# Expert loop of a mixture-of-experts kernel: up projection computed transposed, weights stationary and rows moving, without transposes of the activation

## What is computed

```python
flat = hidden_states.reshape(B * S, H)             # 1536 tokens, H = 192
probs = softmax(flat @ router_w.T)                 # E = 8 experts
topk_probs, topk_idx = top_k(probs, 2)
h = einsum('th,eih->tei', flat, w1)                # up:   192 -> 512
h = silu(h)
outs = einsum('tei,ehi->teh', h, w2)               # down: 512 -> 192
combined = (outs at topk_idx * balanced).sum(axis=1)
```

## Time and profile before

| | us |
|---|---|
| median of 3 runs | 404.68 (402.76 to 408.04) |
| span of the profiled execution | 391.4 |
| first gather of the expert loop | 271.49 |
| first up projection | 276.82 |
| start of the first scatter | 286.54 |
| start of the last scatter | 373.51 |

### The profile page before, as it was taken

How to read it: one execution, slowest core, us unless ns; L and a number is a source line. 1 busy time by engine, 2 the same in 40 slices (tenths; PEclk the granted TensorE clock), 3 DMA queues, 4 the chain that set the end, 5 groups by cost and what they waited for, 6 DMA issues and landing times.

```text
span 391.4 us, 7182 instructions
## 1 busy us (share of the span) xinstructions
PE 254.3 (65%) x2269; PEld 182.2 (47%) x2270; DVE 261.5 (67%) x763; ACT 184.2 (47%) x396; POOL 128.6 (33%) x133
## 2 busy tenths in 40 slices
PE   5986658776443334546656579512899999999800
PEld 3444434444343333435555457501376667667600
DVE  2115568997388898899949976597355555655566
ACT  1131325898798587657526321400255456445401
POOL 3000232554025423303300000012667876866321
PEclk9998556999555565555555555555699999999975
DMA  6000032000004512220100000000211211110046
GB/s 182 6 0 0 1 124 93 3 0 2 2 2 107 121 68 83 80 82 2 32 1 3 7 23 3 30 30 10 62 51 51 69 45 57 53 43 27 26 146 216
DMA packets 12973, 18.98 MB, mean 48 GB/s; under 512 B 3259, under 2 KB 10850, under 8 KB 12434
## 3 DMA queue, kind: packets, MB, share of 16 engines
q1 hardware_dynamic: 9922, 13.90, 11.8%
q0 software_dynamic: 3024, 4.73, 4.1%
HBM read 14.68 MB, written 5.41 MB: 51 GB/s over the span
## 4 chain that ended last, share of the span: by engine, by line
PE 43%; DVE 39%; issue 7%; ACT 6%; DMA 3%; SPq 1%; POOL 0%; DVEq 0%; POOLq 0%; ACTq 0%
DVE at_half L1434 6%; DVE atm L1397 5%; PE bank L891 4%; PE bank L880 3%; PE bank L904 2%; PE bank L906 2%; PE bank L905 2%; PE bank L741 2%; PE bank L876 2%; PE bank L578 2%; PE bank L879 2%; PE bank L878 2%; PE bank L877 2%; DVE v L1320 2%; PE bank L546 2%
## 5 line engine op out<-in xcount | busy, mean ns | idle before, releaser
L480 POOL TENSOR_TENSOR wx<-early,wx 128x1536 f16<-128x1536 f32 (+2 forms) x8 | 28.7, 3584 | 62.6 <-ACT wx L1075 62.6
L1116 ACT ACTIVATE qk<-bank 128x512 f32<-128x512 f32 x31 | 18.5, 597 | 65.1 <-PE bank L880 65.1
L487 POOL DMA_INDIRECT qk<-x_rows,tok_row x32 | 38.6, 1206 | 24.1 <-DVE tok_row L1550 12.8
L741 PE MATMUL bank<-vg,at_half 128*128 128x17 f16 x432 | 13.5, 176 | 40.8 <-DVE at_half L1434 40.8
L492 POOL DMA_INDIRECT y_rows<-qk,dst_row x31 | 31.4, 1013 | 21.7 <-DVE qk L1589 14.9
L1583 DVE COPY qk<-bank 128x512 f16<-128x512 f16 x31 | 13.2, 425 | 33.2 <-PE bank L891 33.2
L741 PEld LDWEIGHTS bank<-vg,at_half 128*128 128x128 f16 x432 | 12.5, 104 | 42.4 <-DVE at_half L1434 27.7
L904 PE MATMUL bank<-wx,qk 128*128 x124 | 30.5, 246 | 0.7 <-DVE qk L1583 0.5
L906 PE MATMUL bank<-wx,qk 128*128 x124 | 30.5, 246 | 0.0
L905 PE MATMUL bank<-wx,qk 128*128 x124 | 30.5, 246 | 0.0
L1056 ACT ACTIVATE at_half<-atm 128x384 f16<-128x384 f32 x48 | 22.5, 518 | 12.9 <-DVE atm L1397 12.9
(11 more groups left out here) (297 smaller groups left out, 737.0 us busy)
## 6 DMA issues: line engine op xcount, KB each, us to landing
early<-in_w SPq DMA_DIRECT2D x4, 768.0 KB, 4.2
early<-in_w1a SPq DMA_DIRECT2D x2, 1024.0 KB, 6.0
early<-in_w1b SPq DMA_DIRECT2D x4, 512.0 KB, 6.3
x_rows<-xr SPq DMA_DIRECT2D x12, 96.0 KB, 1.7
v<-y_rows SPq DMA_DIRECT2D x4, 288.0 KB, 5.0
qk<-y_rows SPq DMA_DIRECT2D x4, 288.0 KB, 5.3
out<-h SPq DMA_DIRECT2D x4, 288.0 KB, 2.9
at_half<-in_wq SPq DMA_DIRECT2D x1, 704.0 KB
```

Source lines behind the costliest of these rows:

```text
L480: pool.tensor_tensor(low, w, high, ALU.subtract).then_inc(s_w_low, 1)
L487: pool.indirect_dma_start(xg[:, i % 4, :], None, x2_dram, bass.IndirectOffsetOnAxis(ap=tok_row[:, i:i + 1], axis=0), bounds_check=NTOK - 1 ...
L741: mm = pe.matmul(bank[6][:, hh * VE:(hh + 1) * VE], at_half[:, a_, i, g, :], vg[:, t * H + hh, v, :], start=(c == 0 and hh == 0 and a_ == ...
```

## The change

`up` is computed transposed. For each of the four blocks of 128 hidden units, the block of weights is stationary and the 128 rows of the slot move: 20 matmuls of 128 columns in place of 5 of 512. The result has hidden units in the partitions and rows in the columns, which is the layout that `down` needs as its stationary operand. So `act_t`, `high_t` and `low_t` go, with `actT`, three semaphores, and PSUM banks 6 and 7 of this stage. `down` takes its operands from `acth` and `actl`. As these buffers are now read by `down`, the second silu and the subtraction of slot i wait for down(i - 2) (`s_down_mm`), and `down` waits for the subtraction. The low half of w1b is computed for 128 partitions, and the last product of `up` uses all 128 (which adds low x low for the last 64 inputs).

```diff
-        parts = {"w1a": (FI, P, W1H, W1L), "w1b": (FI, D - P, W1BH, W1BL), "w2": (MC * D, P, W2H, W2L)}
+        parts = {"w1a": (FI, P, W1H, W1L), "w1b": (FI, P, W1BH, W1BL), "w2": (MC * D, P, W2H, W2L)}
...
                 k %= 2
-                o_ = bank[2 + k][:, :]
-                pe.matmul(o_, xe[:, k, 0:P], w[:, W1H:W1H + FI], start=True, stop=False)
-                pe.matmul(o_, xe[:, k, P:2 * P], w[:, W1H:W1H + FI], start=False, stop=False)
-                pe.matmul(o_, xe[:, k, 0:P], w[:, W1L:W1L + FI], start=False, stop=False)
-                pe.matmul(o_, xe[:, k, 2 * P:3 * P], w[:, W1BH:W1BH + FI], start=False, stop=False)
-                pe.matmul(o_, xe[0:D - P, k, 2 * P:3 * P], w[0:D - P, W1BL:W1BL + FI], start=False, stop=True).then_inc(s_up_mm, 1)
-
-            def act_t(i, k, first=False):
+                for m in range(MC):
+                    o_ = bank[2 + k][:, m * P:(m + 1) * P]
+                    c = m * P
+                    pe.matmul(o_, w[:, W1H + c:W1H + c + P], xe[:, k, 0:P], start=True, stop=False)
+                    pe.matmul(o_, w[:, W1H + c:W1H + c + P], xe[:, k, P:2 * P], start=False, stop=False)
+                    pe.matmul(o_, w[:, W1L + c:W1L + c + P], xe[:, k, 0:P], start=False, stop=False)
+                    pe.matmul(o_, w[:, W1BH + c:W1BH + c + P], xe[:, k, 2 * P:3 * P], start=False, stop=False)
+                    mm = pe.matmul(o_, w[:, W1BL + c:W1BL + c + P], xe[:, k, 2 * P:3 * P], start=False, stop=True)
+                mm.then_inc(s_up_mm, 1)
+
+            def down(i, k, w, first=False):
                 pe.wait_ge(s_low_ready, i + 1)
-                if not first:
-                    pe.wait_ge(s_actT_high, i)
-                    pe.wait_ge(s_actT_low, i)
-                k %= 2
-                for v, half in enumerate((acth, actl)):
-                    ps = bank[6 + v][:, 0:FI // 2].bitcast(F16)
-                    for m in range(MC):
-                        mm = pe.transpose(ps[:, m * P:(m + 1) * P], half[:, k, m * P:(m + 1) * P], ident16[:])
-                mm.then_inc(s_actT_mm, 1)
...
-                    pe.matmul(o_, actT[:, k, 0, c], w[:, W2H + d:W2H + d + D], start=(m == 0), stop=False)
-                    pe.matmul(o_, actT[:, k, 1, c], w[:, W2H + d:W2H + d + D], start=False, stop=False)
-                    mm = pe.matmul(o_, actT[:, k, 0, c], w[:, W2L + d:W2L + d + D], start=False, stop=(m == MC - 1))
+                    pe.matmul(o_, acth[:, k, c], w[:, W2H + d:W2H + d + D], start=(m == 0), stop=False)
+                    pe.matmul(o_, actl[:, k, c], w[:, W2H + d:W2H + d + D], start=False, stop=False)
+                    mm = pe.matmul(o_, acth[:, k, c], w[:, W2L + d:W2L + d + D], start=False, stop=(m == MC - 1))
...
                 act.activation(act32[:, k, :], bank[2 + k][:, :], ACT.Silu, scale=1.0 / WS).then_inc(s_act_ready, 1)
-                act.activation(acth[:, k, :], bank[2 + k][:, :], ACT.Silu, scale=1.0 / WS).then_inc(s_high_ready, 1)
-
-            def high_t(i, k, first=False):
-                act.wait_ge(s_actT_mm, i + 1)
                 if not first:
                     act.wait_ge(s_down_mm, i - 1)
-                act.activation(actT[:, k, 0, :], bank[6][:, 0:FI // 2].bitcast(F16), ACT.Copy).then_inc(s_actT_high, 1)
+                act.activation(acth[:, k, :], bank[2 + k][:, :], ACT.Silu, scale=1.0 / WS).then_inc(s_high_ready, 1)
...
                 if not first:
-                    dve.wait_ge(s_actT_mm, i - 1)
+                    dve.wait_ge(s_down_mm, i - 1)
                 dve.tensor_tensor(actl[:, k, :], act32[:, k, :], acth[:, k, :], ALU.subtract).then_inc(s_low_ready, 1)
-
-            def low_t(i, k, first=False):
-                dve.wait_ge(s_actT_mm, i + 1)
-                if not first:
-                    dve.wait_ge(s_down_mm, i - 1)
-                dve.tensor_copy(actT[:, k, 1, :], bank[7][:, 0:FI // 2].bitcast(F16)).then_inc(s_actT_low, 1)
```

More of the change, by code:

```diff
@@ L330, in build @@
         s_low_ready = sem("low_ready")
-        s_actT_mm = sem("actT_mm")
-        s_actT_high = sem("actT_high")
-        s_actT_low = sem("actT_low")
         s_down_mm = sem("down_mm")
@@ L874, in up @@
                 k %= 2
-                o_ = bank[2 + k][:, :]
-                pe.matmul(o_, xe[:, k, 0:P], w[:, W1H:W1H + FI], start=True, stop=False)
-                pe.matmul(o_, xe[:, k, P:2 * P], w[:, W1H:W1H + FI], start=False, stop=False)
-                pe.matmul(o_, xe[:, k, 0:P], w[:, W1L:W1L + FI], start=False, stop=False)
-                pe.matmul(o_, xe[:, k, 2 * P:3 * P], w[:, W1BH:W1BH + FI], start=False, stop=False)
-                pe.matmul(o_, xe[0:D - P, k, 2 * P:3 * P], w[0:D - P, W1BL:W1BL + FI], start=False, stop=True).then_inc(s_up_mm, 1)
-            def act_t(i, k, first=False):
-                pe.wait_ge(s_low_ready, i + 1)
-                if not first:
-                    pe.wait_ge(s_actT_high, i)
-                    pe.wait_ge(s_actT_low, i)
-                k %= 2
-                for v, half in enumerate((acth, actl)):
-                    ps = bank[6 + v][:, 0:FI // 2].bitcast(F16)
-                    for m in range(MC):
-                        mm = pe.transpose(ps[:, m * P:(m + 1) * P], half[:, k, m * P:(m + 1) * P], ident16[:])
-                mm.then_inc(s_actT_mm, 1)
-            def down(i, k, w, first=False):
-                pe.wait_ge(s_actT_high, i + 1)
-                pe.wait_ge(s_actT_low, i + 1)
+                for m in range(MC):
[8 more added lines that the diff above has]
+            def down(i, k, w, first=False):
+                pe.wait_ge(s_low_ready, i + 1)
                 if not first:
@@ L917, in _ @@
             up(1, 1, w[1], first=True)
-            act_t(0, 0, first=True)
             for i in range(LAG, LEAD):
@@ L921, in _ @@
                 up(i, i % 4, w[i])
-                act_t(i - 1, i - 1)
                 down(i - LAG, (i - LAG) % 4, w[i - LAG], first=(i < 4))
@@ L929, in _ @@
                     up(i, k % 4, w[k - LEAD + LAG])
-                    act_t(i - 1, k - 1)
                     down(i - LAG, (k - LAG) % 4, w[k - LEAD])
-            act_t(NS - 1, NS - 1)
             w = weights(len(WINDOWS) - 1)
@@ L1114, in silu @@
                     act.wait_ge(s_low_ready, i - 1)
-                    act.wait_ge(s_actT_mm, i - 1)
                 act.activation(act32[:, k, :], bank[2 + k][:, :], ACT.Silu, scale=1.0 / WS).then_inc(s_act_ready, 1)
-                act.activation(acth[:, k, :], bank[2 + k][:, :], ACT.Silu, scale=1.0 / WS).then_inc(s_high_ready, 1)
-            def high_t(i, k, first=False):
-                act.wait_ge(s_actT_mm, i + 1)
                 if not first:
                     act.wait_ge(s_down_mm, i - 1)
-                act.activation(actT[:, k, 0, :], bank[6][:, 0:FI // 2].bitcast(F16), ACT.Copy).then_inc(s_actT_high, 1)
-            silu(0, 0, first=True)
-            for i in range(1, LEAD):
+                act.activation(acth[:, k, :], bank[2 + k][:, :], ACT.Silu, scale=1.0 / WS).then_inc(s_high_ready, 1)
+            for i in range(LEAD):
                 silu(i, i % 2, first=(i < 2))
-                high_t(i - 1, (i - 1) % 2, first=(i < 3))
             with act.Fori(0, (NS - LEAD) // 4) as j:
@@ L1131, in _ @@
                     silu(4 * j + k, k % 2)
-                    high_t(4 * j + k - 1, (k - 1) % 2)
-            high_t(NS - 1, (NS - 1) % 2)
             act.wait_ge(s_gate_ready, 2)
@@ L1596, in _ @@
             rows_t(2, 0)
-            low_t(0, 0, first=True)
             low(1, 1, first=True)
@@ L1600, in _ @@
                 rows_t(i + 1, (i + 1) % 2)
-                low_t(i - 1, (i - 1) % 2, first=(i < 3))
                 low(i, i % 2)
@@ L1607, in _ @@
                     rows_t(i + 1, (k + 1) % 2)
-                    low_t(i - 1, (k - 1) % 2)
                     low(i, k % 2)
                     result(i - 2, (k - 2) % 4, rnd=j + (k - 2) // 4)
-            low_t(NS - 1, (NS - 1) % 2)
             for i in range(NS - 2, NS):
```

1 line of the change is left out of this document (removed).

## The result

| | before | after |
|---|---|---|
| median, runs | 404.66 us (402.76 to 408.04), 4 | 422.9 us (421.31 to 424.15), 4 |
| ratio of after to before, 95% interval | | 1.043 [1.0359, 1.0501] |
| span of the profiled execution | 391.4 | 419.5 |
| start of the first and of the last scatter | 286.54, 373.51 | 288.35, 401.48 |
| mean step from scatter to scatter (30 steps) | 2.90 | 3.77 |

The change makes the kernel 18.2 us slower. The prediction was 429.0, range 419 to 446. The spans differ by more than the medians, 28.1 us; the experiments show where that comes from. Medians are of all executions of a kernel, but ratios and their intervals only of those within 1.5% of its fastest, so the two can disagree, and where fewer than three such executions were left the table of experiments has no ratio.

A forecast was written before the change was run, and what follows sets the result against it. TensorE's array looked full before; afterwards its sequencer, with 24 register instructions per iteration, was to set the period. Terms: 24.1 + 1.4 - 1.0 = +24.5 us, span 416, plus 13.3 around it: 429.2 us, range 419 to 446.

The forecast's parts named there:

- The price of a register instruction: On TensorE's sequencer, each instruction that sets a run-time weight offset takes 0.130 us; 24 per iteration after, 12 before.
- the slot of 3.72: One expert-loop iteration after the change: 24 register instructions, 3 additions and 3 waits on TensorE's sequencer, 3.72 us.
- 1.2 us at a boundary: Where TensorE's loop passes read the next experts' numbers: up to 1.2 us each instead of 0.74, +1.4 us in all.
- GpSimd as the bound: Rival: GpSimd's gathers and scatters set the expert loop's period, 2.63 to 2.9 us; about -13 us, 392; chance 0.08.
- The clock: Rival: TensorE's clock falls to half in the expert loop, 449 us if it lasts, 439 if half the time; chance 0.12.
- Unhidden loads: Rival: up's weight loads don't overlap the matmul before, 4.2 us per iteration, +38 us, 443; chance 0.03.
- 13.3 us more, which lies around the span and stays: Outside the profiled span: median 404.68 against span 391.4; added unchanged to the expected span of 416, giving 429.2.
- Start: First two up projections: about +0.5 us for both, offset by the first activation transposes (0.45) that go: nothing.
- Loop with its boundaries: Expert loop on TensorE: +0.83 us on each of 29 iterations, +24.1 us, and +1.4 us at the pass boundaries.
- End: From the last matmul of down 28 to the last scatter's start: about 4.5 us instead of 5.6, so -1.0 us.
- the sequencer story: Main case: TensorE's sequencer sets the loop's period at full clock, 429 us, own bounds 422 to 441; chance 0.72.
- hence hidden: Kernel before: 12 register instructions, additions and waits take the sequencer 2.4 us, under the array's 2.89, so cost nothing.

The follow-up runs named there:

- e1_fixed: Kernel after with the experts' offsets fixed when the program is built, so no register instructions for offsets: 408.25 us, ratio 0.9994 to the kernel before.
- m1_more_rows: Kernel after with a second register for the same offset, used by each block's second matmul: 32 register instructions per slot instead of 24; 461.82 us, ratio 1.1481.
- n1_before_more: Kernel before with a second register for the same offset in up and down: 17 register instructions per slot instead of 12; 418.65 us, ratio 1.0292.
- e2_before_fixed: Kernel before with the experts' offsets fixed when the program is built, so no register instructions for offsets: 405.18 us, ratio 0.9954.
- f1_fixed_flat: As e1_fixed, with the slot loops of TensorE, ScalarE and VectorE written out: 401.23 us, ratio 0.9918 to the kernel before.
- g3_thin: As f1_fixed_flat, with 12 + 8 TensorE matmuls per slot instead of 20 + 12: 397.04 us, ratio 0.9742 to the kernel before.
- b1_before: Kernel before, unchanged, profiled and timed once more: 405.07 us, ratio 1.0009, span of the profile 404.0.

## Why the prediction came out as it did

**Right: the bound.** The price of a register instruction (0.130 forecast, 0.124 measured), the rule that only matmuls with a new offset pay it, up's time (2.1 forecast, 2.20), the loads that hide in 0.056 us (`e1_fixed`), the slot of 3.72 (a median of 3.83 on TensorE), 1.2 us at a boundary (steps of 4.91, 5.07 and 4.75 across the three, 0.9 to 1.2 over the median), GpSimd waiting for DVE, and gathers back at 1.03. `m1_more_rows` is the run that separates this from the other stories, since matmuls, loads and traffic are the same in it.

**The rivals.** GpSimd as the bound would need a register instruction below 0.08 us; even with none of them the mean step was 3.09 to 3.39, and steps of 2.65 us, GpSimd's own pace, came mostly where it caught up after a late result. The clock stayed at 1.00 between 300 and 330 us and was 0.83 in only two stretches of 10 us (330 to 340 and 360 to 370): it was at its lower level, 1.2 GHz, for some 3.4 us in each, and the steps of up around them are 4.07 and 4.09 us, 0.24 and 0.26 over the median. So the clock doesn't set the slot. Unhidden loads are refuted by the rows at 335.36, and in the kernel after itself by the first matmuls behind such a stretch, in which the array had been slower and the sequencer had got ahead:

```profile
339.53 0.22 PE L875 MATMUL bank<-qk,wx 128*128 128x128 f16 x1
...
340.03 0.22 PE L879 MATMUL bank<-qk,wx 128*128 128x128 f16 x1
```

Nine steps in 0.50 us, 0.056 each, with run-time offsets and all loads.

**Wrong: "13.3 us more, which lies around the span and stays".** Around the span lie 1.8 us (the profiled execution of the kernel after took 421.31 with its span of 419.5). The other 11 us were inside: the later executions of the kernel before had spans of 400.4 to 406.6 (but for the one of 718.8), its second profile 404.0, and the execution whose profile I read had none of the waits that the second one has. Its step of 2.90 was the best case; the usual one, by one profile, is 3.24. So the fairer comparison is 3.24 against 3.77, 0.53 us over 30 steps, 15.9 us, beside the 18.2 of the medians; and against the profile that I used it is 2.90 against 3.77 and 28.1 us of span.

**Sizes, against that profile.** Forecast +24.5, measured +28.1. *Start:* the last matmul of up 1 stands at 281.32 before and at 281.36 after, so "nothing" was right. *Loop with its boundaries,* from there to the last matmul of down 28: +28.3 (25.5 forecast). The step is what was too small, 3.72 forecast and 3.83 the median; with the measured 0.124 in place of 0.130 the same sum would have given 3.58. *End,* from there to the last scatter: 5.2 us now instead of 5.6 (-0.4, forecast -1.0).

**Luck in the number.** 429.2 is 6.3 us over the median. The base was 11.5 us too high (13.3 around the span, where 1.8 lie), the sum 3.6 too low, and the profiled execution 1.6 faster than the median of its kernel. These errors cancel in part: 416 for the span, the figure that stands on the rows alone, was 3.5 us under 419.5. The measured median lies near the lower edge, 0.9 us over the 422 that the sequencer story has as its own bound.

**Right, with a condition: "hence hidden".** The cover in the kernel before is the 0.49 us between the sequencer's work and the array's 2.89. `n1_before_more` puts 0.81 on it and pays for what is over. The usual slot is 3.24, and yet the extra 0.35 us of it gave no cover. My reading is that the sequencer stops for late semaphores like everyone else; no run tests that.

**Open:** why the updates are late. They are absent where the slot is longest (`m1_more_rows`, 5.02 us: none of the updates on record comes over 0.4 us after its matmul's start). In the profiles with the least work on the sequencer the mean step stays near 3.1 us (`e2_before_fixed`, `f1_fixed_flat`, `g3_thin`), but the first profile of the kernel before has 2.90, so this is no fixed floor. The trace also lacks records. Of the 512 increments that the landings of 32 gathers give, it holds 496 in the profile of before and 470 in `m1_more_rows`, but 327 in `b1_before`, 350 in the kernel after and 213 in `f1_fixed_flat`. The two don't go together throughout: of the 496 increments of the scatters' landings `m1_more_rows`, where nothing is late, holds 209, and `b1_before` 204; of its 31 updates of down `m1_more_rows` holds some 15. And no instructions were fetched between 316.0 and 374.8 us in `b1_before`, where the waits went on, so it isn't the fetching of instructions. What no run here could vary is the recording itself. The Trainium skill (NOTIFIC — the notification-queue block, section "7.1 Overflow: three behaviours, one of which stalls the engine") describes a mode in which a full queue of records stalls the engine that makes them. In that mode no record is discarded, so the missing ones don't speak for it, and no run here shows it.

The kernel after has late updates too (20.5 us of waits without a name, `b1_before` 34.3), so part of the 18.2 us could be a difference in these. That most of it is the sequencer rests on the undisturbed steps, 2.89 against 3.65 to 3.69, and on `m1_more_rows`, which has none of them.

## What to carry over

Count the register instructions of a loop whose operands sit at run-time offsets, per distinct address and not per matmul: here each was 0.124 us of TensorE's sequencer, so splitting one matmul of 512 columns into four of 128 with their own addresses turned a cover of 0.49 us into a loss of 0.8. Look for them in the steps between loads and in "issue" idle time, not in busy shares, and cut them by operands that span two parts of a tensor. Compare the span of the profiled execution with the spans of the timed ones before adding a term to a median: here the profile was of an execution 9 us shorter than the shortest of 63 others.

## What was not expected of the hardware

- Semaphore updates of TensorE arrived up to 5.9 us (in `e1_fixed`) after the matmul that carries them had started, several of them within 0.35 us, while matmuls behind them were recorded in their usual rhythm. TensorE then stopped. In seven pauses of `e1_fixed` and `f1_fixed_flat`, each of which ended within 0.05 us of the late update, 25 to 30 matmuls, each with its load, had started since the matmul with the missing update. The Trainium skill (TensorE: Matmul & The Clock Gate, section "Architectural detail: the array is 16× 32×32, not 1× 128×128") gives TensorE a queue of 64 instructions; these are 50 to 60, near it. Other pauses came after fewer, and no run here tests whether the queue is what stopped TensorE.
- Two executions of one program differed by 12.6 us of span (391.4 and 404.0) at the same granted clock of 1.00 from 300 to 370 us.
- A register instruction costs the same 0.124 us whether one matmul follows it or two.
